# Two 3x3 convolutions on TensorE: half of the output blocks as one 64x32 product per tap, and their squares split between ScalarE and VectorE

## The reference, cut to what matters

```
x = x + fourier_conv(gn(x), w_real, w_imag, b_real, b_imag)   # layer 0
x = x + gate(gn(x))                                           # layer 1
x = x + conv3x3(gn(x), W2)                                    # layer 2, zero padding 1
x = x + conv3x3(gn(x), W3)                                    # layer 3, zero padding 1
```

## Time and profile before

| | |
|---|---|
| runs, median | 4797.75 us (4794.01 to 4807.09, 3 runs) |
| profiled execution, span | 4801.7 us, its own time to compare with |
| PE busy | 4548.2 us (95%), 84784 matmul records |
| DVE busy | 2925.9 us (61%) |
| ACT busy | 2487.6 us (52%) |
| chain that ended last | PE 91%, of which line 1247 (the two convolutions) 35% of the span |
| the 49104 records of line 1247 | 1728.0 us |

### The profile page before, as it was taken

How to read it: one execution, slowest core, us unless ns; L and a number is a source line. 1 busy time by engine, 2 the same in 40 slices (tenths; PEclk the granted TensorE clock), 3 DMA queues, 4 the chain that set the end, 5 groups by cost and what they waited for, 6 DMA issues and landing times.

```text
span 4801.7 us, 221653 instructions
## 1 busy us (share of the span) xinstructions
PE 4548.2 (95%) x84784; PEld 2936.4 (61%) x84784; DVE 2925.9 (61%) x10604; ACT 2487.6 (52%) x7085; POOL 3.2 (0%) x14
## 2 busy tenths in 40 slices
PE   4999999999999999999999999999999999998889
PEld 1555675556655566556665556655666557655566
DVE  1777717766277662777527765377744777257770
ACT  4455355544555445554455544555445554544435
POOL 0000000000000000000000000000000000000000
PEclk8999999999999899999999989999899999999999
DMA  7443015630166202662036510366004650034304
GB/s 196 111 124 100 4 29 172 176 102 4 47 177 176 79 3 61 178 177 63 4 86 177 176 41 3 105 176 174 24 3 120 177 163 19 3 111 122 90 4 143
DMA packets 290069, 468.11 MB, mean 97 GB/s; under 512 B 25392, under 2 KB 92144, under 8 KB 289264
## 3 DMA queue, kind: packets, MB, share of 16 engines
q1 hardware_dynamic: 289392, 458.29, 33.1%
HBM read 323.98 MB, written 134.22 MB: 95 GB/s over the span
## 4 chain that ended last, share of the span: by engine, by line
PE 91%; DVE 3%; issue 3%; DMA 1%; SPq 1%; ACT 1%; ACTq 0%; DVEq 0%
PE ps L1247 35%; PE ps L1165 19%; PE ps L1150 18%; PE ps L1158 6%; PE ps L1174 5%; PE ps L1024 5%; DMA x<-x 1%; PE ps L1273 1%; PE ps L1070 1%; PE ps L1071 0%; PE ps L1097 0%; PE ps L1305 0%; PE ps L1219 0%; SPq L360 0%; PE ps L1112 0%
## 5 line engine op out<-in xcount | busy, mean ns | idle before, releaser
L1247 PE MATMUL ps<-x,conv_s 32*32 32x512 f32 x49104 | 1728.0, 603 | 20.8 <-DVE x L948 16.7
L1247 PEld LDWEIGHTS ps<-x,conv_s 32*32 32x32 f32 x49104 | 1252.8, 103 | 437.9 <-issue 196.1
L563 ACT ACTIVATE x<-ps,vec 128x256 f32 (+1 forms) x1024 | 492.0, 495 | 1003.1 <-PE ps L1165 1003.1
L1165 PE MATMUL ps<-hil,shared 128*128 128x256 f32 x4096 | 993.6, 386 | 0.0
L814 DVE COPY vsb<-ps 128x512 f32<-128x512 f32 x512 | 329.9, 686 | 1043.6 <-PE ps L1150 1043.6
L1165 PEld LDWEIGHTS ps<-hil,shared 128*128 128x128 f32 x4096 | 740.2, 190 | 273.8 <-issue 194.1
L802 DVE SCALAR_TENSOR_TENSOR shared<-xin,trig 128x256 f32<-128x256 f32 x2048 | 821.6, 441 | 57.3
L629 ACT ACTIVATE x<-ps,vec 64x512 f32<-64x512 f32 (+1 forms) x768 | 527.2, 686 | 395.9 <-PE ps L1247 385.6
L1150 PE MATMUL ps<-shared 32*32 32x512 f32 x16384 | 656.4, 605 | 0.0
L620 ACT ACTIVATE x<-ps,vec 128x512 f32 x512 | 347.9, 685 | 439.6 <-PE ps L1247 439.6
L1150 PEld LDWEIGHTS ps<-shared 32*32 32x32 f32 x16384 | 306.2, 104 | 280.0 <-issue 216.8
(11 more groups left out here) (170 smaller groups left out, 2720.6 us busy)
## 6 DMA issues: line engine op xcount, KB each, us to landing
xin<-x SPq DMA_DIRECT2D x512, 256.0 KB
out<-x SPq DMA_DIRECT2D x512, 256.0 KB
shared<-x SPq DMA_DIRECT2D x448, 256.0 KB, 5.0
shared<-t_strip SPq DMA_DIRECT2D x512, 96.0 KB, 3.6
x<-x SPq DMA_DIRECT2D x64, 256.0 KB, 8.1
x<-t_proj SPq DMA_DIRECT2D x1, 2048.0 KB, 11.8
hil<-t_hil SPq DMA_DIRECT2D x1, 560.0 KB, 12.1
trig<-t_trig SPq DMA_DIRECT2D x1, 512.0 KB, 11.8
```

The lines of the kernel that those rows point to most:

```text
L563: ins = nc.scalar.activation(split_in(strip_of(s))[:, q, :], split_in(ps[:, bank, :])[:, q, :], ACT.Identity, bias=v1(MEAN), accum_out=sum ...
L1165: mm = pe.matmul(split_in(ps[:, BY + 2 * odd + e, :])[:, int(q < 2), :], xt[:, e, q, :], hil[:, q, 0:HALF], start=False, stop=True, skip_g ...
L1247: mm = pe.matmul(ps[TM * cg:TM * cg + TM, banks[k], :], conv_s[TM * rg:TM * rg + TM, kw, second, :], x1[TM * rg:TM * rg + TM, of, kw:kw + ...
```

## The change

Every second block of a strip has its two row groups within partitions 0 to 63 or 64 to 127 of the same strip. These blocks now take one product of 64x32 per tap (`whole`), with both halves of the weights one above the other. The other blocks keep two products of 32x32 (`parts`). The weight table `conv_w` has the same size: its index that told first from second now tells WHOLE from APART. A slot thus issues 4 first parts, 4 whole products and 4 second parts of the earlier pair, 12 products for the 16 of before. The compiled program marks the whole products with a tile size of 64x32 and the parts with 32x32.

The squares of layer 2: the first strip of each pair is squared by ScalarE right behind its two evictions, the second by VectorE, both straight into `cols`; `red` and its copies are gone.

```
+                def whole(p, banks, outputs, kw):
+                    for k in range(2):
+                        for cg, (of, rg), _ in outputs(2 * p + k)[0]:
+                            rows = slice(TM * rg, TM * rg + HP)
+                            pe.matmul(ps[TM * cg:TM * cg + TM, banks[k], :], conv_s[rows, kw, WHOLE, :], x1[rows, of, kw:kw + N],
+                                      start=(kw == 0), stop=(kw == TAPS - 1), skip_group_check=True)
+
+                def parts(p, banks, outputs, second, kw):
+                    for k in range(2):
+                        for cg, *operands in outputs(2 * p + k)[1]:
+                            if operands[second] is not None:
...
-                    return [(m, m, ((s, (m - 1 + at) % TILES) if m else before, (s, (m + at) % TILES))) for m in range(TILES)]
+                    of = [(m, (s, (m - 1 + at) % TILES) if m else before, (s, (m + at) % TILES)) for m in range(TILES)]
+                    return of[1::2], of[0::2]
...
-                        taps(n, PAIRS - 1 - n, banks2(n), outputs2, 0, kw)
+                        parts(PAIRS - 1 - n, banks2(n), outputs2, 0, kw)
+                        whole(PAIRS - 1 - n, banks2(n), outputs2, kw)
...
-                        taps(n, PAIRS - 1 - n, banks2(n), outputs2, 1, kw)
+                        parts(PAIRS - 1 - n, banks2(n), outputs2, 1, kw)
...
-                    taps(n, n, banks3(n), outputs3, 0, kw)
+                    parts(n, banks3(n), outputs3, 0, kw)
+                    whole(n, banks3(n), outputs3, kw)
...
+                    act.wait_ge(evicted, ev(i, 1 + 2 * n + 1))
+                    act.wait_ge(a_c_squared, i * PAIRS + n + FREE)
+                    nc.scalar.activation(junk, strip_of(STRIPS - 2 - n * 2), ACT.Square,
+                                         accum_out=cols[:, 3, bass.ds(STRIPS - 2 - n * 2, 1)]).then_inc(a_c_squared, 1)
...
-                    for k in range(GROUP):
-                        s = j * -GROUP + (STRIPS - 2 - 2 * (k // 2) + k % 2)
+                    for k in range(GROUP // 2):
+                        s = j * -GROUP + (STRIPS - 1 - 2 * k)
...
-                                               accum_out=red[:, k:k + 1]).then_inc(c_squared, 1)
-                    dve.wait_ge(c_squared, i * STRIPS + j * GROUP + GROUP + 2)
-                    V.tensor_copy(cols[:, 3, bass.ds(j * GROUP, GROUP)], red[:, 0:GROUP]).then_inc(c_reduced, 1)
+                                               accum_out=cols[:, 3, bass.ds(s, 1)]).then_inc(c_squared, 1)
```

More of the change, by code:

```diff
@@ L53, with second_block @@
 AXB, AXC, AXS = 0, 1, 2
+WHOLE, APART = 0, 1
+def second_block(rg, kind):
+    return (rg + kind) % 2
 ZR = 96
@@ L112, in tables @@
     eye_conv = np.zeros((P, 2, TAPS, 2, TM))
-    for rg in range(TILES):
+    for rg, kind in itertools.product(range(TILES), range(2)):
         for c in range(C):
-            eye_conv[TM * rg + C + c, :, 1, 0, c] = 1.0
-            eye_conv[TM * rg + c, :, 1, 1, C + c] = 1.0
+            if second_block(rg, kind):
+                eye_conv[TM * rg + c, :, 1, kind, C + c] = 1.0
+            else:
+                eye_conv[TM * rg + C + c, :, 1, kind, c] = 1.0
     zsel = np.zeros((ZR, P + ZR))
@@ L162, in placed @@
         for kw in range(TAPS):
[L163 to L170, removed]
+            for rg, kind, r, o in itertools.product(range(TILES), range(2), range(2), range(2)):
+                kh = 2 * second_block(rg, kind) + r - o
+                if 0 <= kh < 3:
+                    for c in range(C):
+                        convs[TM * rg + C * r + c, l, kw, kind, C * o:C * o + C] = wt[:, c, kh, kw]
     return {"w_mix": mix, "w_u": uw, "w_bias": bias, "w_conv": convs}
@@ L311, in program @@
         pads_zeroed, v_pads, pair_due, halved = sem("pads_zeroed"), sem("pads3_ready"), sem("conv_pair_due"), sem("conv_pair_halved")
-        convolved, evicted, c_squared, c_reduced = sem("convolved"), sem("evicted"), sem("c_squared"), sem("c_reduced")
+        a_c_squared = sem("a_c_squared")
+        convolved, evicted, c_squared = sem("convolved"), sem("evicted"), sem("c_squared")
         v_sums3, p_stat3, v_conv3, p_bias3, v_bias3 = sem("sums3"), sem("pe_stat3"), sem("conv3_weights"), sem("pe_bias3"), sem("bias3")
@@ L979, in image @@
                     squares(j)
-                dve.wait_ge(c_reduced, u0 + GROUPS + FREE)
-                dve.wait_ge(c_squared, (i + 1) * STRIPS + 2)
+                dve.wait_ge(a_c_squared, i * PAIRS + PAIRS + FREE)
+                dve.wait_ge(c_squared, (i + 1) * PAIRS + 2)
                 c.did(V.memset(cols[0:C, 2, 0:1], 0.0))
-                c.then(V.memset(cols[0:C, 3, STRIPS - 2:STRIPS - 1], 0.0))
+                c.then(V.memset(cols[0:C, 3, 0:1], 0.0))
                 for q in (2, 3):
@@ L1238, in convolutions @@
                     prepare_h(i + 1)
-                def taps(n, p, banks, outputs, second, kw, done=None):
+                def whole(p, banks, outputs, kw):
                     for k in range(2):
-                        for m, cg, operands in outputs(2 * p + k):
+                        for cg, (of, rg), _ in outputs(2 * p + k)[0]:
[5 more added lines that the diff above has]
+                        for cg, *operands in outputs(2 * p + k)[1]:
                             if operands[second] is not None:
                                 of, rg = operands[second]
+                                rows = slice(TM * rg, TM * rg + TM)
                                 only = operands[1 - second] is None
-                                mm = pe.matmul(ps[TM * cg:TM * cg + TM, banks[k], :], conv_s[TM * rg:TM * rg + TM, kw, second, :],
-                                               x1[TM * rg:TM * rg + TM, of, kw:kw + N], start=(kw == 0 and (second == 0 or only)),
-                                               stop=(second == 1 and kw == TAPS - 1), skip_group_check=True)
+                                mm = pe.matmul(ps[TM * cg:TM * cg + TM, banks[k], :], conv_s[rows, kw, APART, :], x1[rows, of, kw:kw + N],
+                                               start=(kw == 0 and (second == 0 or only)), stop=(second == 1 and kw == TAPS - 1), skip_group_check=True)
                     if kw == TAPS - 1:
@@ L1321, in second3 @@
                         due()
-                    taps(n, n, banks3(n), outputs3, 1, kw)
+                    parts(n, banks3(n), outputs3, 1, kw)
                 prepare_at = dict(zip(U_AT + C_AT, (prepare_u1, prepare_u2, column_parts, column_turn, column_sums)))
```

15 lines of the change are left out of this document (7 added, 8 removed).

## The result

The changed kernel takes 6430.78 us (median of 4 runs, 6429.85 to 6432.01), the kernel before 4802.42 us on the same chip (median of 4, 4794.01 to 4809.0). The ratio is 1.3395, with a 95% interval of 1.3376 to 1.3414. The forecast was 6257: the sign and the mechanism came as told, and 174 us are missing from the sum. Five of them are the kernel before, which the forecast counts from at 4797.75 us and which here took 4802.42; of the change itself 1628 us were measured and 1459 forecast.

The account below looks back on a forecast made before the run. The prediction took TensorE's convolutions as the bound. Slots of 1.99 us add 1464 us over eight images, less 3 and 2: +1459 on 4801.7, 6261, put at 6257 against the median; range 5850 to 6650.

Parts of the forecast that it names:

- The stop at each change of shape: TensorE, layers 2 and 3: each switch between 32x32 and 64x32 stops the array, making two phases a slot, 1.99 us.
- the lengths of 1.08 and 1.05 us: Phase lengths assumed in a slot: 1.08 us for eight parts, 1.05 for four whole products, each less 0.07 overlap.
- The 0.86 us for which a product holds its sub-array: TensorE: each product was said to occupy its sub-array for 0.86 us, which the change leaves as it is.
- The whole array stops: TensorE: a new shape was said to wait for all sub-arrays, not just its own, until 0.07 us before the end.
- the second rival: TensorE: a shape change waits for its own sub-arrays only; 276 us more, 5075 us in all; chance 0.05.
- The first rival: TensorE: no stop between 32x32 and 64x32, fewer products pack better; up to 261 us saved, 4660 us; chance 0.10.
- the third rival: TensorE's clock falls: over 9000 us at 1.2 GHz throughout, some 6520 if in a tenth of the slots; chance 0.04.
- The sum: Whole kernel: slower slots +1464 us, idle time swallowed in the last layer 3 -3, squares -2; together +1459.
- the slot: Layers 2 and 3: a slot goes from 1.05 and 1.02 to 1.99 us, +90 and +93 us an image.
- a clock that falls for a while: TensorE: a temporary clock drop, given no term but allowed for by widening the range to 5850 to 6650 us.
- The squares and the waits: Layer 2: sharing squares between ScalarE and VectorE gives -2 us in all; TensorE's waits are met earlier or still met.

## Why the prediction was right

**The stop at each change of shape** was right, and nearly to the number. Blocks overlap by 0.07 us, loads stand for 0.84, a slot is 2.01 for 1.99; the lengths of 1.08 and 1.05 us that were taken between two rows came out as 1.09 and 1.06. The TensorEngine Tiling (Array Packing) page of the Trainium skill, section Key Properties, says both that a change of the tiling mode drains TensorE and that tiles of one mode work independently. Both halves held here: layer 2 takes 210.90 us with six changes a pair, and 105.60 with the same work in one shape. The 0.86 us for which a product holds its sub-array held as well (5.15 us for six in the run with 64x32 alone), though the earlier trace rows bear it out only in part: the three rounds of sixteen there take 3.40 us (800.80 to 804.20), and 1.15 + 2 x 0.86 would be 2.87.

**The whole array stops**, not only the sub-arrays that the next product wants. Parts and whole products of layer 2 never share a sub-array and still run one after the other. With the second rival a pair would have been about 3.6.

**The first rival** (no stop, 4660 us) would have needed blocks that overlap, and there are none. Its other half, that fewer products pack better, stays open: no run has twelve products of this layout without a stop. By its own terms its time would be 4667 us rather than 4660, and that of the third rival, a low clock throughout, 6257 + (3.7 - 1.99) x 192 x 8 = 8880 rather than over 9000; neither changes an argument.

**The sum** was short by 174 us, about 11% of the change. Its terms, as measured:
- the slot, 0.02 x 192 slots x 8 images = 31 us, a size a little off;
- the odd block, 39 us, by the run that moved it. The sum had no term for it. The kernel shows it on row group 1 and column group 0, where one of the first parts stands too, and that was not looked up;
- the granted clock at the start of both layers, 111 us, by the run that filled it. The third rival asked whether the clock falls in the whole convolution or in a tenth of it. It fell in the part where a phase has four products instead of eight, which the prediction did not tell apart from the rest; a clock that falls for a while stood in the range.

The three are 181 us; 6257 + 181 = 6438 against 6431. They come from different chips, and the odd block's share is measured at half clock, so they are not quite independent. The middle of the layers kept its clock at 1.00, so the forecast's picture of one steady slot was right there and wrong at the edges.

**The squares and the waits** cost nothing, as forecast: the squares alone gain 3 us by the medians, and in the changed kernel this view of waits of layer 2 (who waits <- for whom: us in all, times, longest), which answers to the earlier trace rows:

```profile
DVE work L973 <- ACT x L628: 145.6, 31, 20.9
ACT x L628 <- PE ps L1263: 131.3, 31, 13.2
```

Both wait for TensorE, and longer than before (ScalarE 54.0 us).

## What to carry to other kernels

On a TensorE stream of small tiles, count the changes of shape before the products: the array ran one shape at a time here, each change cost 0.145 us, and what used to run beside was put behind. After a change in how such a stream is packed, look at its first microseconds apart from the steady part: a thin start held the clock at its lower level here, and a few useless products were cheaper than none. In the old order, where the start was fuller, they gained nothing.

## What the runs showed that was not expected

- TensorE reads as busy for 5.00 of 5.00 us and is granted 0.50 of its clock for more than 20 us. With four more 32x32 products in each phase of parts, on sub-arrays that stood idle, it was low for 3.4 us instead of the 17.1 of the same kernel without them. The busy share of the page doesn't show the difference between the two; the records in a stretch do (30 against 62).
- A product whose sub-array is taken waits for it even when the rest of the array is empty, and a phase with a stop at its end makes all others wait with it: one misplaced small product cost 1.68 us each time.
- An added increment of a semaphore on TensorE's queue cost 0.09 us in layer 2 of the images inside the loop and 0.03 in the last two, outside it. Why is open.
- With 64x32 alone, a pair ran at the 5.16 us of its deepest sub-arrays (5.15). With 32x32 alone it runs at 3.13 for 2.57. What makes up this gap is open: the doubled increments show that the queue between the products can stretch a pair, but taking one away in every second pair shortened none. So is whether fewer records are a part of it.
